# Decoder layer on one core: first projections in halves, first tiles on two queues, engine orders in the head groups

## What is computed

```python
q = split(hidden_states @ Wq.T + bq)
k = split(hidden_states @ Wk.T + bk)
v = split(hidden_states @ Wv.T + bv)
scores = jnp.einsum('bhsd,bhtd->bhst', q, k)
scores = (scores + bias[None]) / math.sqrt(HD)
scores = 30.0 * jnp.tanh(scores / 30.0)
scores = jnp.where(causal[None, None], scores, -jnp.inf)
probs = jax.nn.softmax(scores, axis=-1)
ctx = jnp.einsum('bhst,bhtd->bhsd', probs, v)
...
x = x + _L0_attn_ref(_layernorm(x, axis=-1), ...)
x = x + _L0_xattn_ref(_layernorm(x, axis=-1), ctx_2048, mask_BxS2_bk0)
x = x + _L0_ffn_ref(_layernorm(x, axis=-1), ...)
```

## Time and profile before

| | |
|---|---|
| runs shown | 563.09, 563.39, 561.78 us; median 563.09 |
| the profiled execution | 563.1 us, of which its span is 561.0 |
| PE busy | 547.0 us, 97% of the span |
| DVE, ACT, POOL busy | 352.7, 268.0, 286.4 us |
| mean granted clock of PE | 0.994 |
| DMA | 50.74 MB, mean 90 GB/s |

### The profile page before, as it was taken

How to read it: one execution, slowest core, us unless ns; L and a number is a source line. 1 busy time by engine, 2 the same in 40 slices (tenths; PEclk the granted TensorE clock), 3 DMA queues, 4 the chain that set the end, 5 groups by cost and what they waited for, 6 DMA issues and landing times.

```text
span 561.0 us, 10139 instructions
## 1 busy us (share of the span) xinstructions
PE 547.0 (97%) x3946; PEld 428.9 (76%) x3946; DVE 352.7 (63%) x701; ACT 268.0 (48%) x485; POOL 286.4 (51%) x258
## 2 busy tenths in 40 slices
PE   8999999989989999999999999999999999999997
PEld 7787888768868888888888888766686667866675
DVE  7997877895676667578787885345633564244422
ACT  6747976856845687567744352033401333023310
POOL 4297798965494554996794336324400343013320
PEclk9999999989989999999999999999999999999999
DMA  8951231452123520129571902200001000100001
GB/s 295 339 212 39 78 96 56 150 190 77 39 77 94 171 56 3 58 69 285 204 270 55 302 3 92 77 0 1 1 37 39 0 1 0 58 19 1 0 20 56
DMA packets 43422, 50.74 MB, mean 90 GB/s; under 512 B 2544, under 2 KB 25072, under 8 KB 43376
## 3 DMA queue, kind: packets, MB, share of 16 engines
q1 hardware_dynamic: 43376, 50.10, 27.2%
HBM read 36.46 MB, written 13.63 MB: 89 GB/s over the span
## 4 chain that ended last, share of the span: by engine, by line
PE 83%; POOL 7%; DVE 5%; ACT 2%; issue 2%; DMA 1%; DVEq 0%; ACTq 0%; POOLq 0%
PE bank L287 34%; PE bank L433 23%; PE bank L453 16%; PE bank L282 2%; PE bank L375 2%; PE bank L360 2%; POOL x_res L735 2%; PE bank L385 2%; POOL q_w L721 2%; POOL q_w L719 2%; POOL probs L712 1%; DVE q_m L1200 1%; PE bank L352 1%; POOL reduced L704 1%; ACT kT L856 1%
## 5 line engine op out<-in xcount | busy, mean ns | idle before, releaser
L287 PE MATMUL bank<-reduced 128*128 128x512 f32 x936 | 226.0, 398 | 3.5 <-DVE x_res L1167 2.6
L287 PEld LDWEIGHTS bank<-reduced 128*128 128x128 f32 x936 | 175.2, 190 | 42.2 <-issue 4.9
L814 POOL TENSOR_TENSOR f_parts<-fused,f_parts 128x512 fp32r<-128x512 f32 x48 | 62.9, 1310 | 159.3 <-ACT f_parts L1047 159.3
L1029 ACT ACTIVATE tanh_g<-bank,half_gate 128x512 f32<-128x512 f32 x48 | 33.0, 688 | 150.8 <-PE bank L433 139.2
L453 PE MATMUL bank<-reduced,f_parts 128*128 128x512 f32 x384 | 88.4, 390 | 0.0
L453 PEld LDWEIGHTS bank<-reduced,f_parts 128*128 128x128 f32 x384 | 71.8, 188 | 15.0
L1361 DVE SCALAR_TENSOR_TENSOR silu<-tanh_g,bank 128x512 f32<-128x512 f32 x48 | 32.9, 685 | 64.0 <-ACT tanh_g L1029 63.9
L433 PE MATMUL bank<-reduced 128*128 128x512 f32 x288 | 72.0, 402 | 0.0
L433 PEld LDWEIGHTS bank<-reduced 128*128 128x128 f32 x288 | 54.1, 188 | 12.9
L712 POOL TENSOR_SCALAR_AFFINE_SELECT probs<-probs 128x1024 f32<-128x1024 f32 x32 | 36.9, 1160 | 44.9 <-ACT probs L881 44.9
L719 POOL TENSOR_TENSOR q_w<-q_w,q_m 128x512 f32<-128x512 f32 x36 | 49.3, 1370 | 10.2 <-DVE q_m L1202 10.2
(11 more groups left out here) (123 smaller groups left out, 725.8 us busy)
## 6 DMA issues: line engine op xcount, KB each, us to landing
quantized<-q_w SPq DMA_DIRECT2D x36, 256.0 KB, 3.3
reduced<-quantized SPq DMA_DIRECT2D x12, 512.0 KB, 7.0
memT_sb<-in_memT SPq DMA_DIRECT2D x16, 256.0 KB, 5.0
mem_sb<-in_mem SPq DMA_DIRECT2D x16, 256.0 KB, 5.6
out<-y_sb SPq DMA_DIRECT2D x16, 256.0 KB, 2.0
q_w<-in_gate_w SPq DMA_DIRECT2D x12, 256.0 KB, 3.1
q_w<-in_up_w SPq DMA_DIRECT2D x12, 256.0 KB, 3.2
x_res<-in_x SPq DMA_DIRECT2D x3, 1024.0 KB, 9.3
```

What stands on the lines that cost most here:

```text
L287: ins = pe.matmul(dst, stationary, moving, start=(n == 0), stop=(n == len(pairs) - 1))
L814: pool.tensor_tensor(f_lo[:, f, :], fused[:, f % 2, :], f_hi[:, f, :].bitcast(F32), ALU.subtract).then_inc(f_lo_ready, 1)
L1029: act.activation(tanh_g[:, f % 2, :], src[:], ACT.Tanh, scale=half_gate[:, f:f + 1]).then_inc(tanh_ready, 1)
```

## The change

- `first_qk` makes Q and K in halves of two tiles each: high by high, high by low and low by high of tiles 0 and 1 for Q and K in turn, then the same of tiles 2 and 3. Its products have 256 columns. Tile 3 is transposed after the first four products. `keep_busy` before the four transposes goes from 11, 2, 1, 2 to 10, 1, 1.
- SP loads tiles 0 and 2, ACT's queue tiles 1 and 3. POOL computes the shifts of tiles 0 and 1.
- In the head ACT makes the high part of the K weights before those of tiles 2 and 3; DVE makes tiles 2 and 3 in turn with the low parts, and the distance tables of head groups 1 to 3 after two more weight parts. scores(0, 0) waits for the first table alone.
- At the end of hg 2 tile 2 is transposed into bank Q and tile 3 into bank K; ACT drains Q before K and makes the high parts of two tiles before `context_high`.
- In hg 2 DVE applies the norm to one tile of group g - 1 before `x_low`, and to three after it. In hg 1 `wo_out` 2 goes before a slab. In hg 3 the statistics are split around the cross attention's step.
- In hg 0 of groups 2 and 3, ACT's second exp goes before the second part of cross step 3.

The diff, cut to its core:

```diff
--- before.py
+++ after.py
@@ -324,29 +324,48 @@
                     (w_hi[:, m, k, n], xT_hi[:, k]), (w_hi[:, m, k, n], xT_lo[:, k]),
...
-            def first_qk(name):
-
-                m = "QK".index(name)
-                dst, done = take((name, 0, 0), (Q_BANK, K_BANK)[m])
-                pe.wait_ge(w_hi_made, m + 1)
+            def first_qk():
+
+                banks = [take((name, 0, 0), (Q_BANK, K_BANK)[m]) for m, name in enumerate("QK")]
+
+                def part(m, cols, w, t, start=False, stop=False):
+                    dst, done = banks[m]
+                    for k in range(KT):
+                        ins = pe.matmul(dst[:, cols], w[:, m, k, FIRST], t[:, k, cols], start=start and k == 0,
+                                        stop=stop and k == KT - 1)
+                    return ins, done
+
+                first, second = slice(0, 2 * S), slice(2 * S, TG)
+                pe.wait_ge(xT_hi_ready, 2)
+                for m in range(2):
+                    pe.wait_ge(w_hi_made, m + 1)
+                    part(m, first, w_hi, xT_hi, start=True)
+                    if m == 0:
+                        turn_x(0, 3, S_BANK + 3)
+                for i in range(2):
+                    wait_drained(pe, ("N", 0, i))
+                for m in range(2):
+                    part(m, first, w_hi, xT_lo)
+                for m in range(2):
+                    pe.wait_ge(w_lo_made, m + 1)
+                    part(m, first, w_lo, xT_hi, stop=True)
                 pe.wait_ge(xT_hi_ready, GT)
-                for k in range(KT):
-                    pe.matmul(dst[:], w_hi[:, m, k, FIRST], xT_hi[:, k], start=(k == 0), stop=False)
-                pe.wait_ge(w_lo_made, m + 1)
-                for k in range(KT):
-                    pe.matmul(dst[:], w_lo[:, m, k, FIRST], xT_hi[:, k], start=False, stop=False)
-                for i in range(GT):
+                for m in range(2):
+                    part(m, second, w_hi, xT_hi, start=True)
+                for m in range(2):
+                    part(m, second, w_lo, xT_hi)
+                for i in range(2, GT):
                     wait_drained(pe, ("N", 0, i))
-                for k in range(KT):
-                    ins = pe.matmul(dst[:], w_hi[:, m, k, FIRST], xT_lo[:, k], start=False, stop=(k == KT - 1))
-                ins.then_inc(done, 1)
+                for m in range(2):
+                    ins, done = part(m, second, w_hi, xT_lo, stop=True)
+                    ins.then_inc(done, 1)
...
                 dst = [take(("S", g, hg, j), S_BANK + j) for j in range(4)]
-                if g == 0 and hg == 0:
-                    pe.wait_ge(bias_made, 2 * HG)
+                if g == 0 and hg < 2:
+                    pe.wait_ge(bias_made, 2 * HG if hg else 2)
                 for j in range(4):
...
                     pe.matmul(dst[j][0][:], bias_l[rows, hg, :],
@@ -472,12 +491,11 @@
                     pe.matmul(bank[E_BANK][:, 0:P], identity[:].bitcast(F32), identity[:].bitcast(F32), start=True, stop=True)
...
             pe.wait_ge(identity_made, 1)
-            for i, n in enumerate((11, 2, 1, 2)):
+            for i, n in enumerate((10, 1, 1)):
                 keep_busy(n)
...
             keep_busy(3)
-            first_qk("Q")
-            first_qk("K")
+            first_qk()
             for g in range(G):
...
                 qk_proj("Q", g, 1)
@@ -507,7 +525,7 @@
                 qk_proj("Q", g, 3)
...
                 for i in range(GT):
-                    turn_x(g + 1, i, (S_BANK, S_BANK + 1, K_BANK, Q_BANK)[i])
+                    turn_x(g + 1, i, (S_BANK, S_BANK + 1, Q_BANK, K_BANK)[i])
                 if g == G - 1:
...
                 context(g, 2)
@@ -570,7 +588,8 @@
                 sp.dma_start(raw[m].rearrange("p (k n) -> p k n", k=KT)[:, :, cols],
...
-            for i in range(GT):
+
+            for i in range(0, GT, 2):
                 sp.dma_start(x_res[:, i, :], x_t[:, i, :]).then_inc(x_first_loaded[i], 16)
...
             weights(0)
@@ -741,6 +760,10 @@
                 pool.wait_ge(eps_added[0], i + 1)
...
                     .then_inc(first_rstd, 1)
+                if i < 2:
+                    pool.wait_ge(first_rstd, i + 1)
+                    pool.tensor_scalar(shift[:, i:i + 1], mv[0][:, i, 0:1], rstd[0][:, i:i + 1], -1.0, ALU.mult, ALU.mult)\
+                        .then_inc(shift_made, 1)
...
             pool.wait_ge(small_loaded, 16)
@@ -939,14 +962,17 @@
                 act.activation(xn1[:, i, :], token_tile(0, i), ACT.Identity, bias=shift[:, i:i + 1],
...
+            x_t = x.rearrange("b s d -> s b d")
+            for i in range(1, GT, 2):
+                act.dma_start(x_res[:, i, :], x_t[:, i, :]).then_inc(x_first_loaded[i], 16)
             norm_first(0)
...
             weight_high(0)
+            weight_high(1)
             x_high(0, 2)
             x_high(0, 3)
-            weight_high(1)
             weight_high(2)
...
             act.wait_ge(small_loaded, 16)
@@ -962,9 +988,10 @@
                     cross(g - 2, 2)
...
                     k_out(g, 1)
-                    cross(g - 2, 3)
+                    cross_first(g - 2, 3)
+                    exp(g, 0, 2)
+                    cross_second(g - 2, 3)
                     cross_first(g - 2, 4)
-                    exp(g, 0, 2)
                 else:
...
                     heads(g, 0, 2)
@@ -999,10 +1026,11 @@
...
                 heads(g, 2, 2)
+                q_out(g, 3)
                 k_out(g, 3)
-                q_out(g, 3)
-                context_high(g, 1)
-                for i in range(GT):
+                for i in range(GT):
+                    if i == 2:
+                        context_high(g, 1)
                     x_high(g + 1, i)
...
@@ -1214,11 +1242,6 @@
             dve.tensor_scalar(bits_i[:, 1:2], part_i[:], 2, 1, ALU.bitwise_and, ALU.logical_shift_right).then_inc(bits_made, 1)
...
             dve.tensor_copy(odd[:], bits_i[:]).then_inc(bits_cast, 1)
-            def first_shift(i):
-                dve.wait_ge(first_rstd, i + 1)
-                dve.tensor_scalar(shift[:, i:i + 1], mv[0][:, i, 0:1], rstd[0][:, i:i + 1], -1.0, ALU.mult, ALU.mult)\
-                    .then_inc(shift_made, 1)
-
             for i in range(GT):
...
                 norm_stats(0, 0, i, token_tile(0, i))
@@ -1226,29 +1249,36 @@
                 dve.bn_aggr(mv[0][:, i, :], bn[0][:, i, :]).then_inc(var_ready[0], 1)
...
                 dve.tensor_scalar(var_eps[0][:, i:i + 1], mv[0][:, i, 1:2], EPS, None, ALU.add).then_inc(eps_added[0], 1)
-                if 1 <= i < 3:
-                    first_shift(i - 1)
-
-            dve.wait_ge(xn_ready[0], 2)
-            for i in range(2, GT):
+
+            def norm_late(i):
                 dve.wait_ge(first_rstd, i + 1)
+                if i == 2:
+                    dve.wait_ge(xn_ready[0], 2)
                 dve.tensor_scalar(xn1[:, i, :], token_tile(0, i), mv[0][:, i, 0:1], rstd[0][:, i:i + 1],
                                   ALU.subtract, ALU.mult).then_inc(xn_ready[0], 1)
-            x_low(0, 0)
-            x_low(0, 1)
-            weight_low(0)
-            x_low(0, 2)
-            x_low(0, 3)
-            weight_low(1)
-            dve.wait_ge(slope_step, 9)
-            dve.wait_ge(place_made, 1)
-            for hg in range(HG):
+
+            def distances(hg):
                 dve.tensor_scalar(bias_l[:, hg, :], place_n[:], even[:, 0:1], in_left[:, hg:hg + 1], ALU.mult, ALU.add)\
...
                     .then_inc(bias_made, 1)
-            for n in range(2, V_PART + 1):
-                weight_low(n)
+
+            norm_late(2)
+            x_low(0, 0)
+            norm_late(3)
+            x_low(0, 1)
+            weight_low(0)
+            weight_low(1)
+            x_low(0, 2)
+            x_low(0, 3)
+            dve.wait_ge(slope_step, 9)
+            dve.wait_ge(place_made, 1)
+            distances(0)
+            weight_low(2)
+            weight_low(3)
+            for hg in range(1, HG):
+                distances(hg)
+            weight_low(V_PART)
             dve.wait_ge(small_loaded, 16)
...
             dve.tensor_tensor(fuse_c[:], gate_c[:], up_c[:], ALU.mult).then_inc(fuse_c_made, 1)
@@ -1267,12 +1297,13 @@
                     dve.scalar_tensor_tensor(ctxT[:], rows, bv_c[:, k:k + 1], ctxT[:], ALU.mult, ALU.add)\
...
-            def next_stats(g):
-                if g < G:
+            def next_stats(g, tiles=range(GT)):
+                if 0 in tiles and g < G:
                     dve.wait_ge(x_group_loaded[g], 16)
-                for i in range(GT):
+                for i in tiles:
                     norm_stats(0, g, i, token_tile(g % G, i))
-                norm_moments(0, g)
+                if GT - 1 in tiles:
+                    norm_moments(0, g)
...
                 if g:
@@ -1314,8 +1345,8 @@
                     wo_out(g - 1, 0)
...
                     wo_out(g - 1, 1)
+                    wo_out(g - 1, 2)
```

(8 more changed lines are left out.)

## The result

The changed kernel takes 558.1 us (median of 6 runs, 556.5 to 558.5) beside 563.1 us before (6 runs, 561.8 to 564.6): the ratio is 0.990, with an interval of 0.988 to 0.992. It is 5.0 us faster where 9.8 were forecast, and the time lies outside the range. The profiled execution took 558.2 us with a span of 556.4, so the two traces differ by 4.9 us and can be laid beside each other.

The account below looks back on a forecast made before the run. PE, busy 547.0 of 561.0 us, bounds the kernel; only its standstill or lower clock can be won. 0.7 + 1.6 + 0.5 + 2.4 + 1.6 + 1.5 + 1.5 = 9.8 us, from 563.1 to 553.3, range 551.2 to 557.2.

Parts of the forecast that it names:

- What the three moved `norm_apply` delay: Group 1, DVE: they delay normalize_context (1, 2), needed after the next two projections; some 1 to 2 us are left.
- rival 3: Group 1: the stall is replaced, Q(2, 0) or context(1, 3) waiting for DVE; 4.0 us not won, 557.3 us; chance 0.05.
- sign of being wrong: Anywhere after the head: a PEclk of 0.50 would show the prediction wrong; no size given.
- The head: Before the first heads' scores: scores(0, 0) starts 0.7 us sooner, ends from 1.2 sooner to 3 later.
- the cost of the halves: Head: 48 products of 256 columns cost 0.12 us each, 5.8 us again; upper end 0.19 each.
- the 0.4 for tile 0: Head loads: with two queues tile 0 lands 0.4 us later, between 0 and 0.67.
- The shift on POOL: Head: shifts moved from DVE to POOL bring tile 1 0.3 us sooner, with 0 and 0.5 as ends.
- The transposes: End of head group 2: one tile's transposes, 0.54 us, leave the path; 1.6 us won in groups 0, 2, 3.
- Group 1: Masks limit the transposes' gain to 0.5 us; the 2.4 us wait before scores(1, 3) and 1.6 of clock go.
- Group 2: Wait for cross 6's residual: POOL's chain moves 1.5 us, 1.1 us stay without clock fall, winning 1.5 more.
- The clock: After the long waits in groups 1 and 2: two falls to 1.2 GHz go, winning 1.6 and 1.5 us.
- lower end: Whole kernel: 551.2 us, with the head's best end and the whole wait of group 2 gone.

Follow-up runs that it names:

- experiment 1: Changed kernel with all four norm_apply ahead of the low parts again in the last group only: 553.8 us, ratio 0.984.
- 2: Kernel before, in the last group only one norm_apply ahead of the low parts and three behind: 563.3 us, ratio 1.001.
- 3: Changed kernel with context_high ahead of the four high parts again in the last group, the norm_apply split kept: 554.4 us.
- 4: Kernel before, in the last group only norm_apply split one and three, and context_high behind two high parts: 563.8 us, ratio 1.002.
- experiment 8: Kernel of experiment 1 with the second half's products in the order Q, Q, Q, K, K, K: 553.6 us.
- Experiment 7: Kernel of experiment 1 with everything ahead of the first scores as in the kernel before: 554.6 us against 553.8.
- Experiment 6: Kernel of experiment 1 with ACT's second exp of head group 0 back behind cross step 3 and the first part of step 4: 556.9 us.
- Experiment 10: Kernel of experiment 1 with ACT's high part of the fourth context ahead of mem_hi of cross step 4 in groups 2 and 3: 554.5 us.

## Why the prediction was right and wrong

- **The step that failed** is the last part of the paragraph on group 1, "What the three moved `norm_apply` delay", together with `context_high` behind two high parts, which the prediction priced at nothing. It followed DVE through group 1 only, and rival 3 also looked for the loss there. Its sign of being wrong, a PEclk of 0.50 after the head, did come, at 272 to 276 us. The edit stands under a loop over groups, and the last one is different: DVE waits there for the flag sum, which used to cover the four instructions and had 1.70 us to spare. Behind the wait they are exposed, and there is no next group to take up the delay, as the cross step feeds the feed-forward part. Cost: 2.3 + 0.2 us of wait and 1.9 us of lower clock, 4.4 in the traces; experiment 1 wins back 4.3. The other terms of the sum hold but for the head: 9.05 us of 9.8 were won ahead of this place.
- **What I would not have found in the rows of before even so:** neither edit alone makes the wait (2, 3), both together do (4). PE reaches the transpose of the cross step 18.04 us after context (3, 2) in the kernel before, and needs `x_sc` to start 1.27 us ahead of it, so there was room for 16.8 us. `x_sc` came after 14.84, 1.9 us to spare. The split needs 16.5 and fits; the two edits need 19.2, 2.4 too many, and the waits are 2.27 + 0.18. `context_high`, now later on ACT, puts POOL's work beside DVE's `norm_apply`, and their 0.67 us put `q_m` beside the masks. That POOL's work beside them is what stretches DVE's instructions is read from the rows of these kernels; no experiment takes POOL's work away.
- **The head.** 0.7 us forecast, 0.11 in the traces. Right were the cost of the halves (44 products in 5.50 us, 0.125 each, so at these widths width sets the price and not the number) and the 0.4 for tile 0 (it was 0.48). The first is luck in part: the rows given for it are 72 products of one width, which cannot show it. `k_out` starts at 16.59, where 15.9 was forecast and 16.70 stood before. Three things make the difference. The shift on POOL took 0.24 us off the way from tile 0's statistics to the normalisation of tile 1 (3.15 instead of 3.39), not 0.3, so the 0.48 for tile 0 was only half cancelled, and the first product starts at 10.02, not 9.75. From it to the bias products it is 6.28 us, where 6.15 were added up. And `k_out` starts 0.29 us behind the bias products instead of 0.11, as `q_out`, which used to run beside K's products, starts only at 16.00 and is in its way: 0.18, as much as experiment 8 wins back. Experiment 7 gives 0.3 to 0.8 for the head as a whole, so the total is not settled.
- **The transposes.** Right: sixteen take 1.49 us instead of 2.06.
- **Group 1.** Right: the masks of POOL bound context (1, 2), which waits 0.70 us for them and starts 1.15 us sooner, of which 0.69 were there already; the 2.4 us wait and the fall are gone, and PE did not wait anew in head group 3.
- **Group 2.** Right to a tenth: 1.13 us of wait are left of 2.58, and 72 products take 16.58 us instead of 18.07. Experiment 6 gives the 1.5 us by which POOL's chain moves (its low part starts at 142.78 in experiment 1 and at 144.29 in experiment 6). Experiment 10 confirms the chain (ACT's high part, POOL's low part, slabs, residual): moved another 1.7 us forward (the low part at 142.97, with the head 1.9 us later), it removes the rest. That 1.1 us of wait brings no fall was a guess between 0.6 and 2.4; it came true here, but 1.22 us in the head were followed by one in experiment 10.
- **The clock.** 3.1 of the 9.8 us were two falls seen in one profile. That is right for the profile. As a forecast for a median it is uncertain: by their mean clocks, runs of the same kernel before had from none to three of them. Where the third lies, no profile shows.
- **The range.** Its lower end, 551.2, is not what its two terms give: 553.3 - 0.5 - 1.1 = 551.7.

## What to carry to other kernels

An edit inside a loop over groups is priced in each group, above all in the first and the last, whose neighbours differ: an instruction that stood ahead of a wait was free, and behind it it is not. Where a stretch of an engine nearly reaches a deadline, add up all edits that lengthen it, and count what another engine does to its instructions if it is moved beside them. Where a wait can be followed by a fall of the clock, compare runs of like mean clock before concluding from medians.

## What the runs showed of the hardware

- A fall to 1.2 GHz does not follow a wait of given length for certain. Waits of 2.27 us (the changed kernel) and 2.40 us (the kernel before) were followed by one, waits of 2.25 and 2.40 us in experiment 4 were not, and in the head one of 1.22 us was (experiment 10). The Trainium skill ("TensorE: Matmul & The Clock Gate", What's actually happening) says that the chip's watch on activity runs freely and is not started by the kernel; that agrees with falls that come and go from run to run.
- The first tile lands later and less regularly when two queues load at once: by 0.5 us on average, with a spread of 0.64 us (8 profiles) in place of 0.22 (6 profiles). No run separates the sharing of the engines from the order of the issues.
- A DVE instruction of 0.42 us (`q_m`, input and output in SBUF) takes 1.2 to 1.5 us beside POOL's. Size is no protection: `x_w` (L1191, 128x1, two inputs in SBUF) takes 0.16 us in nine of its sixteen places in the changed kernel and 1.25 us at 154.25, beside a POOL instruction of 1.26 us from 154.23 on, and there the residual that PE waits for stands right behind it. In the changed kernel the two lines of `q_m` sum to 31.5 + 35.1 us, in the kernel before to 26.4 + 32.7: 7.5 of the 9 us that DVE is busier.
